# Three-layer relational graph convolution: two of three layers with more dense node ranges, gather ring of eight groups

## The chip, the cores and the metric

The kernel runs on one core of a Trainium2 chip. A core has TensorE (PE, matrix products; PEld is its weight load), VectorE (DVE), ScalarE (ACT), GpSimd (POOL) and SyncE (SP), which work in parallel and wait for each other through semaphores, and 16 DMA engines. The metric is the device time of one execution in microseconds (us); lower is better.

## The reference

There are 6250 nodes with 128 features, 100000 edges of four types, sorted by destination (the destinations are denser at low node numbers), and three layers:

```python
def _rgcn_conv(x, edge_index, edge_type, W, root, bias):
    src, dst = (edge_index[0], edge_index[1])
    x_src = x[src]
    out = x @ root + bias
    for r in range(N_REL):
        mask = (edge_type == r).astype(x.dtype)
        s = jax.ops.segment_sum(x_src * mask[:, None], dst, num_segments=N_NODES)
        c = jax.ops.segment_sum(mask, dst, num_segments=N_NODES)
        mean = s / jnp.maximum(c, 1.0)[:, None]
        out = out + mean @ W[r]
    return out
...
for l in range(N_LAYERS - 1):
    x = _rgcn_conv(x, edge_index, edge_type, weights[l], roots[l], biases[l])
    x = jax.nn.relu(x)
x = _rgcn_conv(x, edge_index, edge_type, weights[-1], roots[-1], biases[-1])
return x
...
x = _layernorm(x + _L0_gnn_ref(edge_index, edge_type_4, x, L0_gnn_weights, L0_gnn_roots, L0_gnn_biases), axis=-1)
```

## The kernel before

The edges lie in tiles of 128 and groups of four tiles, 196 groups in all, the nodes in 49 blocks of 128. A group's edges reach few nodes, since the destinations are sorted. There are two ways to sum a group.

**Sparse.** GpSimd fetches the rows of x times W for the edges of a tile by an indirect DMA (L724) from the table `ytab` in DRAM into `ring`, which holds `R` = 9 groups. Gather group n waits until TensorE has used group n - R (L720). VectorE builds the weighted one-hot matrices `S` (L1347), and TensorE multiplies (L888, items "S", eight matmul records to a group) into `psGR` or `psRB`. VectorE adds the sums to `node` (L1369, items "A").

**Dense.** The first groups, whose edges fall on few nodes, are put together to windows of at most 116 destination nodes. `WINDOWS` says how many windows each layer sums densely: 5, 9 and 9, that is groups 0 to 57 in the first layer and 0 to 76 in the others. A window's matrix A counts the edges between every source node and its destination nodes, per type. TensorE multiplies the split features `xs` by A (L970, 98 products of 512 columns to a window, items "C" in 25 pieces of two blocks), and then by the weights (L913, item "G"). Marker items in between are "M" (the counts broadcast by L905 and copied by ScalarE at L1081), and "F" (the product of both at L1500). A window is **built** in the first layer that uses it: bins from its edges (items "P": L1378 to L1382 on VectorE, L939 and L941 on TensorE), then per block one-hots (L1397, L1398 on VectorE), their product (L986) and a copy (L1070), and every two blocks a conversion to 16 bits (L1074) and a store to `a_dram`. In later layers the window is **loaded**: 13 chunks of up to 512 KB go through the two slots of `aring` (issue L630 on SyncE, after the slot's last chunk has been converted), and ScalarE converts each in two pieces (L1046) into `afull`. The first layer builds windows 0 to 4, the second loads these and builds 5 to 8, the third loads all nine. Loaded windows alternate between the banks `psD` and `psB` (the table `second`); built windows all use `psD`, since `psB` then holds the bins of the next one.

**Preparation.** Before the layers, VectorE ranks the edges of the windows in phases of about 100 tiles (`rank_counts`, `rank_scan`, `rank_places`, L1160 to L1215): windows 0, then 1 to 3, then 4 to 8. Behind the last phase it sets a flag (L1330), for which all engines wait in `branch`. Before the flag GpSimd gathers only the first R groups.

**What sets the order.** `schedule` writes one list of items per layer from planned costs, and all engines follow it in order. It takes `R`, the number of windows and their groups. A loaded piece of two blocks costs 0.88 us of TensorE in its table, which has no term for the loads. `pace` spreads the dense items so that they end some 100 us ahead of the gathers, and it is at least 1. Items "E" (the next layer's table, `relu` and `root` products) and "L" (the layer norm and output) go in between as soon as their nodes are complete. A layer's first gather waits until the table is stored (`y_stored`).

Of the kernel before, what the change touches and what calls it, by code (L numbers as in the profile page):

```python
# [17 lines left out]
P = 128  # L18
D = 128
NR = 4  # L20
# [1 line left out]
RW = 1024  # L22
FAR = 1000000
EPS = 1e-5
WINDOWS = (5, 9, 9)
SPAN = 116
START_PE, START_POOL = 205.0, 95.0
BANK = 4
# [5 lines left out]
class Plan:  # L34
# [3 lines left out]
    def __init__(self, N, E):  # L38
# [9 lines left out]
        g = 0  # L48
        while len(self.win) < max(WINDOWS):
            h = g  # L50
# [14 lines left out]

        self.W = [min(w, len(self.win)) for w in WINDOWS]
        self.G1 = [self.win[w - 1][1] for w in self.W]
# [40 lines left out]

def schedule(pl, R):

# [24 lines left out]
    for li in range(NL):  # L135
# [58 lines left out]
        def step_pool():  # L194
            nonlocal pool
            n = len(arrive)
            if n >= NS or (n >= R and n - R >= len(eaten)):
                return False
            pool = max(pool, eaten[n - R] if n >= R else 0.0) + ntile[n] * gather
            arrive.append(pool + land)  # L200
# [72 lines left out]
def rgcn_kernel(nc, x, src, dst, typ, weights, roots, biases, c_ident, c_iota, c_tri, c_col, c_need,  # L273
# [3 lines left out]
    NP, NG, NT, NB, NSL, TH = pl.NP, pl.NG, pl.NT, pl.NB, pl.NSL, pl.TH  # L277
    NT4 = NP * 8
    NW = NB * P + P
    NK = NR * N  # L280
    R = 9
    NS = 6
    SHEAD = 3
    YS = 4
# [6 lines left out]
    NPB = 2  # L291
# [13 lines left out]
    width = [c * NB for _, _, c in pl.win]  # L305
    layers = schedule(pl, R)

# [74 lines left out]
    with ctx:  # L382
        sb = lambda name, shape, dt=F32: ctx.enter_context(nc.sbuf_tensor(name, shape, dt))
# [36 lines left out]
        bt = sb("bt", [P, NL])  # L420
        ring = sb("ring", [P, R * 512])
        S = sb("S", [P, NS, 4, P])
# [11 lines left out]
        WB = W * NB  # L434
        OH = NO * (1 + NR) * P // 2
        PBW = P + max(width)
        V = sb("V", [P, max(NR * P + OH + NPB * 4 * PBW, 4 * WB + 5 * TH + 4 * (NP + 2))])
        cap, tot, offs, adj = (V[:, i * WB:(i + 1) * WB] for i in range(4))
        blk, tmpi, tmp2 = (V[:, 4 * WB + i * TH:4 * WB + (i + 1) * TH].bitcast(I32) for i in range(3))
        relw = V[:, 4 * WB + 3 * TH:4 * WB + 4 * TH]  # L440
        ident16 = V[:, 4 * WB + 4 * TH:4 * WB + 4 * TH + P // 2].bitcast(F16)
        rowt = V[0:2, 4 * WB + 5 * TH:4 * WB + 5 * TH + 4 * (NP + 2)].rearrange("r (a b c) -> r a b c", a=2, b=2)
        ms = V[:, 0:NR * P]
        oh = V[:, NR * P:NR * P + OH].bitcast(F16).rearrange("p (v c) -> p v c", v=NO)
        ohs, ohk = oh[:, :, 0:P], oh[:, :, P:(1 + NR) * P]
# [54 lines left out]
        q = {n: sem(n) for n in names}  # L500
        s_ring = [sem(f"s_ring{i}") for i in range(R)]
        s_yd = [sem(f"s_yd{i}") for i in range(YS)]
# [1195 lines left out]
```

## Time and profile before

| what | us |
|---|---|
| median of 3 runs | 2216.3 |
| their range | 2212.05 to 2216.36 |
| the profiled execution | 2218.82 |
| its span, first to last instruction | 2217.0 |
| GpSimd busy | 1556.1 (70%) |
| TensorE busy | 1591.0 (72%) |
| VectorE busy | 1239.0 (56%) |
| ScalarE busy | 1002.8 (45%) |

The span is that of one profiled execution; the profile's page gives busy times, the chain of work that ended last, and groups of instructions by source line. In a row, "<-" behind a bracketed number names what ended the idle time before the instruction; "issue" means that nothing in the profile held it. Busy time of TensorE counts pipelined products by modelled ends.

### The profile page before, as it was taken

The page shows a single profiled execution, that of the slowest core. Times are in us where ns is not written, and L with a number is a line of the kernel's source. Part 1 is how long each engine was busy: PE and PEld are TensorE (multiplying, and loading weights), DVE is VectorE, ACT ScalarE, POOL GpSimd, SP SyncE. Part 2 cuts the span into 40 slices and gives each one's busy share as a digit, 9 for nine tenths or more (in the row PEclk, how much of TensorE's full clock was granted, in tenths as well). Part 3 has the DMA queues.
Part 4 walks back from the last instruction along what each step waited for, and adds up shares of the span by engine and source line. Part 5 has one row for each costly group of instructions (what it writes and reads, how often), then busy time and mean ns, then how long its engine had stood idle before and what let it go on. Part 6 is the DMA issues. An engine that isn't in the chain of part 4 may idle for free.

```text
span 2217.0 us, 27610 instructions
## 1 busy us (share of the span) xinstructions
PE 1591.0 (72%) x7831; PEld 1130.9 (51%) x7831; DVE 1239.0 (56%) x4096; ACT 1002.8 (45%) x1499; POOL 1556.1 (70%) x1506
## 2 busy tenths in 40 slices
PE   6612768888898886558899887787476777777743
PEld 3301434555565554337677555554255566656532
DVE  4887988989876753223248766563133233433343
ACT  4400002446676771146667675683244454544200
POOL 0182887777777777747777777777477777777774
PEclk9855667989998996679999899998679988999855
DMA  6300122323444453257774444454465555656331
GB/s 206 136 29 18 59 67 73 115 97 133 134 160 136 162 172 112 86 189 231 218 222 149 142 156 133 151 173 146 126 216 169 168 181 178 198 186 188 119 87 49
DMA packets 164847, 314.28 MB, mean 142 GB/s; under 512 B 34816, under 2 KB 85120, under 8 KB 164692
## 3 DMA queue, kind: packets, MB, share of 16 engines
q1 hardware_dynamic: 113096, 210.74, 27.8%
q0 software_dynamic: 47936, 98.12, 15.9%
q10 hardware_dynamic: 3660, 3.60, 0.6%
q8 instruction: 67, 1.10, 0.2%
q14 instruction: 88, 0.72, 0.1%
HBM read 206.52 MB, written 105.80 MB: 141 GB/s over the span
## 4 chain that ended last, share of the span: by engine, by line
POOL 49%; issue 18%; DVE 15%; PE 9%; DMA 5%; ACT 1%; DVEq 1%; ACTq 1%; SPq 0%; POOLq 0%
POOL ring L724 49%; DMA aring<-a_dram 2%; PE psY L764 2%; DVE V L1398 2%; DVE S L1347 2%; DMA ring<-ytab,idxc 2%; DVE V L1397 2%; DVE V L1382 1%; PE psD L970 1%; DVE rows L1197 1%; PE psT L764 1%; PE psRB L888 1%; DVEq L1355 1%; ACT afull L1046 1%; DVE node L1369 1%
## 5 line engine op out<-in xcount | busy, mean ns | idle before, releaser
L724 POOL DMA_INDIRECT ring<-ytab,idxc x1498 | 1553.1, 1037 | 639.5 <-issue 449.0
L970 PE MATMUL psD<-afull,xs 128*128 128x512 f32 (+1 forms) x1666 | 572.8, 472 | 59.6 <-ACT afull L1046 33.1
L1347 DVE TENSOR_SCALAR S<-iota,relc,wc 128x128 f32<-128x128 f32 x1498 | 418.4, 365 | 114.5 <-PE psGR L888 74.3
L1046 ACT ACTIVATE afull<-aring 128x1024 fp32r<-128x1024 f16 (+1 forms) x350 | 346.0, 1032 | 213.7 <-DMA aring<-a_dram 139.1
L970 PEld LDWEIGHTS psD<-afull,xs 128*128 128x128 f32 (+1 forms) x1666 | 330.8, 205 | 130.0 <-issue 32.6
L888 PE MATMUL psRB<-S,ring 128*128 128x128 f32 x1516 | 246.3, 313 | 178.6 <-DMA ring<-ytab,idxc 171.4
L888 PE MATMUL psGR<-S,ring 128*128 128x128 f32 x1480 | 241.6, 316 | 175.5 <-DMA ring<-ytab,idxc 158.1
L888 PEld LDWEIGHTS psRB<-S,ring 128*128 128x128 f32 x1516 | 220.7, 220 | 219.2 <-issue 178.0
L888 PEld LDWEIGHTS psGR<-S,ring 128*128 128x128 f32 x1480 | 218.6, 223 | 213.7 <-issue 167.8
L1074 ACT ACTIVATE aring<-afull 128x1024 f16<-128x1024 f32 (+1 forms) x225 | 234.0, 1040 | 21.0 <-ACT afull L1070 0.7
L1070 ACT ACTIVATE afull<-psT 128x512 fp32r<-128x512 f32 x295 | 171.5, 593 | 115.7 <-PE psT L986 113.5
L1397 DVE TENSOR_SCALAR V<-iota,recs 128x128 f16<-128x128 f16 x588 | 157.4, 268 | 101.3 <-PE psT L986 58.2
L1398 DVE TENSOR_SCALAR V<-iota,recs 128x512 f16<-128x512 f16 x588 | 209.8, 357 | 0.0
L970 PE MATMUL psB<-afull,xs 128*128 128x512 f32 (+1 forms) x588 | 159.2, 416 | 6.0 <-ACT afull L1046 6.0
L986 PE MATMUL psT<-V 128*128 128x512 f16 x389 | 142.4, 405 | 6.5 <-DVE V L1398 6.3
L1369 DVE TENSOR_TENSOR node<-node,psRB 128x128 f32 x199 | 57.2, 287 | 154.6 <-issue 72.6
L1053 ACT ACTIVATE xs<-xst 128x512 fp32r<-128x512 f32 (+1 forms) x39 | 23.2, 595 | 266.2 <-DMA xst<-in_x 243.9
L1369 DVE TENSOR_TENSOR node<-node,psGR 128x128 f32 x200 | 57.4, 287 | 126.7 <-DVE node L1369 63.1
L970 PEld LDWEIGHTS psB<-afull,xs 128*128 128x128 f32 (+1 forms) x588 | 110.6, 198 | 31.1 <-ACT afull L1046 7.8
L999 ACT ACTIVATE yst<-psT 128x512 f32<-128x512 f32 x66 | 39.2, 595 | 185.0 <-PE psT L764 184.9
L1070 ACT ACTIVATE afull<-psY 128x512 fp32r<-128x512 f32 x146 | 86.4, 592 | 61.6 <-PE psY L986 60.8
L764 PE MATMUL psY<-wt,node 128*128 128x512 f32 (+1 forms) x162 | 94.9, 671 | 22.4 <-DVE node L1487 14.1
(197 smaller groups left out, 1470.4 us busy)
## 6 DMA issues: line engine op xcount, KB each, us to landing
aring<-a_dram SPq DMA_DIRECT2D x168, 512.0 KB
a_dram<-aring SPq DMA_DIRECT2D x108, 512.0 KB
ytab<-yst SPq DMA_DIRECT2D x144, 256.0 KB
ring<-ytab,idxc POOLq DMA_INDIRECT x1498
hrows<-yst SPq DMA_DIRECT2D x96, 64.0 KB
xst<-hrows SPq DMA_DIRECT2D x24, 256.0 KB
xst<-in_x SPq DMA_DIRECT2D x12, 256.0 KB
yst<-in_x SPq DMA_DIRECT2D x11, 256.0 KB, 4.2
```

The costliest lines, as they stand in the source:

```text
L724: e.indirect_dma_start(ring[0:m, at:at + P], None, Y[li % 2], bass.IndirectOffsetOnAxis(ap=idxc[0:m, t:t + 1], axis=0)).then_inc(s_ring[n ...
L764: e.matmul(y_bank(li, k)[0:bw[k], :], h, wt[:, li].rearrange("i r o -> i (r o)"), start=True, stop=True).then_inc(q["s_ym"], 1)
L888: last = e.matmul(o, ring[0:m, at:at + P], S[0:m, n % NS, i, :], start=(i == 0), stop=(i == len(tiles[g]) - 1))
L970: last = e.matmul(bank[:], xs[0:m, s, i, :], a, start=(i == 0 and s == 0), stop=(i == NB - 1 and s == 1))
L986: e.matmul(tbank(u)[:], ohs[:, v % NO, :], ohk[:, v % NO, :], start=(j == 0), stop=(j == c - 1)).then_inc(q["s_bd"], 1)
L1046: e.activation(afull[:, n % AF, 0:m, :], aring[:, cc % AS, o:o + m, :], ACT.Copy).then_inc(q["s_cv"], 1)
L1070: e.activation(afull[:, n % AF, j, :], tbank(u)[:], ACT.Copy).then_inc(q["s_tA"], 1)
L1074: e.activation(aring[:, cc % AS, half:half + m, :], afull[:, n % AF, 0:m, :], ACT.Copy).then_inc(q["s_cv"], 1)
L1347: last = e.tensor_scalar(S[:, n % NS, i, :], iota[:], relc[:, t:t + 1], wc[:, t:t + 1], ALU.is_equal, ALU.mult)
L1369: e.tensor_tensor(w, w, part[bank][:, j * P:(j + 1) * P], ALU.add).then_inc(q["s_acc"], 1)
L1397: e.tensor_scalar(ohs[:, v % NO, :], iota16[:, 0:P], recs[:, 0, at:at + 1], None, ALU.is_equal)
L1398: e.tensor_scalar(ohk[:, v % NO, :], iota16[:], recs[:, 1, at:at + 1], None, ALU.is_equal).then_inc(q["s_oh"], 1)
```

## The change

The dense windows become 5, 10 and 13, and the ring 8 groups. With `SPAN` unchanged the new windows are windows 9 to 12, which hold groups 77 to 80, 81 to 84, 85 to 88 and 89 to 91. The first layer still uses windows 0 to 4. The second loads 0 to 4 and builds 5 to 9; the third loads 0 to 9 and builds 10 to 12. Sparse groups are 138, 115 and 104 instead of 138, 119 and 119; tiles 550, 458 and 414 instead of 550, 474 and 474. The edges of windows to be ranked grow from 308 to 368 tiles, and the preparation has a fourth phase with windows 9 to 12. The rest of the diff packs `ident16` and `rowt` closer in the buffer `V`.

```diff
-WINDOWS = (5, 9, 9)
+WINDOWS = (5, 10, 13)
...
-    R = 9
+    R = 8
...
-        V = sb("V", [P, max(NR * P + OH + NPB * 4 * PBW, 4 * WB + 5 * TH + 4 * (NP + 2))])
+        V = sb("V", [P, max(NR * P + OH + NPB * 4 * PBW, 4 * WB + 4 * TH + P // 2 + 4 * (NP + 2))])
...
-        rowt = V[0:2, 4 * WB + 5 * TH:4 * WB + 5 * TH + 4 * (NP + 2)].rearrange("r (a b c) -> r a b c", a=2, b=2)
+        rowt = V[0:2, 4 * WB + 4 * TH + P // 2:4 * WB + 4 * TH + P // 2 + 4 * (NP + 2)].rearrange("r (a b c) -> r a b c", a=2, b=2)
```

On VectorE, in the preparation behind the third ranking phase (L1213 is its last step, L1312 the first step towards the flag), the difference of the two orders begins so:

```order
 L1213 SCALAR_TENSOR_TENSOR colc<-V 128x16
+L1165 MEMSET rows 128x1470
+L1166 TENSOR_TENSOR rows<-V,iota 128x2940
+L1171 TENSOR_REDUCE V<-rows 128x49 x4
+L1185 COPY V<-psGR 128x196
+L1186 TENSOR_TENSOR V<-V 128x196
+L1188 TENSOR_TENSOR V<-psGR,V 128x196
+L1192 TENSOR_TENSOR V<-V 128x195
+L1194 CAST rows<-V 128x49 x4
+L1197 SCALAR_TENSOR_TENSOR rows<-rows 128x2940
+L1198 TENSOR_TENSOR rows<-rows 128x2940
```

A whole phase is added, over 60 tiles (2940 = 49 x 60), between the third and the flag.

On TensorE, in the third layer, from the product by the weights for one loaded window (L913) towards the next window's counts (L905), before:

```order
L913 MATMUL psGR<-V,wt 128x128 x4
L888 MATMUL psRB<-S,ring 128x128 x4
L970 MATMUL psD<-afull,xs 128x512 x8
L888 MATMUL psRB<-S,ring 128x128 x4
L970 MATMUL psD<-afull,xs 128x512 x12
L888 MATMUL psRB<-S,ring 128x128 x4
L970 MATMUL psD<-afull,xs 128x512 x12
L888 MATMUL psRB<-S,ring 128x128 x4
L970 MATMUL psD<-afull,xs 128x512 x8
```

And after, at the same place of the layer:

```order
L913 MATMUL psRB<-V,wt 128x128 x4
L888 MATMUL psRB<-S,ring 128x128 x4
L970 MATMUL psD<-afull,xs 128x512 x20
L888 MATMUL psRB<-S,ring 128x128 x4
L970 MATMUL psD<-afull,xs 128x512 x16
L888 MATMUL psRB<-S,ring 128x128 x4
L970 MATMUL psD<-afull,xs 128x512 x20
```

Between two gather groups (L888) there stand 16 to 20 dense products (L970) where 8 to 12 stood. From one window's counts to the next there are six groups instead of eleven: M0 to M9 stand at groups 4, 10, 16, 22, 28, 33, 39, 45, 51 and 57, where M0 to M8 stood at 11, 22, 33 and so on to 96. In the second layer M4 moves from group 34 to group 30.

## Rows read from the trace of the kernel before

**Rows 1.** Page, the chain that ended last, share of the span by engine.
```profile
POOL 49%; issue 18%; DVE 15%; PE 9%; DMA 5%; ACT 1%; DVEq 1%; ACTq 1%; SPq 0%; POOLq 0%
```

**Rows 2.** Waits of GpSimd: us in total, times, longest us.
```profile
POOL ring L724 <- issue: 449.0, 1473, 0.3
...
POOL ring L724 <- PE psGR L888: 42.5, 8, 40.3
```

**Rows 3.** Gathers alone, first layer: length, POOL busy (instructions), clock, DMA share, GB/s.
```profile
220.00:941.00 721.00, 564.18 (x514) 0.84 0.36 115
```

**Rows 4.** Timeline, GpSimd, at the layers' ends: start, us, instruction, [idle <-releaser].
```profile
220.45 1.50 POOL L724 DMA_INDIRECT ring<-ytab,idxc  x1 [40.33 <-PE psGR L888]
...
964.35 0.95 POOL L724 DMA_INDIRECT ring<-ytab,idxc  x1 [23.37 <-DMA hrows<-yst]
...
1575.70 0.87 POOL L724 DMA_INDIRECT ring<-ytab,idxc  x1 [0.30 <-issue]
1601.65 0.95 POOL L724 DMA_INDIRECT ring<-ytab,idxc  x1 [25.09 <-DMA hrows<-yst]
...
2195.36 0.87 POOL L724 DMA_INDIRECT ring<-ytab,idxc  x1 [0.30 <-issue]
```

**Rows 5.** Timeline, third ranking phase in the preparation, VectorE and TensorE.
```profile
169.60 2.10 DVE L1165 MEMSET rows<- 128x2450 uint32 x1 [0.58 <-DVE colc L1213]
171.62 5.20 DVE L1166 TENSOR_TENSOR rows<-V,iota 128x4900 uint8<-128x4900 int32 x1
176.86 5.50 DVE L1171 TENSOR_REDUCE V<-rows 128x49 f32<-128x1176 uint8 x5
...
187.10 10.37 DVE L1197 TENSOR_TENSOR_SCAN rows<-rows 128x4900 f16<-128x4900 f16 x1
197.50 5.26 DVE L1198 TENSOR_TENSOR rows<-rows 128x4900 f16<-128x4900 f16 x1
202.88 4.27 PE L808 MATMUL psGR<-rows,V 128*128 128x100 f16 x49 [18.42 <-DVEq L1199]
...
208.21 0.54 DVE L1213 SCALAR_TENSOR_TENSOR colc<-V 128x24 f32<-128x24 int32 x5
```

**Rows 6.** Timeline, ScalarE, second layer: the marks of windows 0, 1, 2, 4.
```profile
1013.40 0.60 ACT L1081 ACTIVATE V<-psT 128x512 f32<-128x512 f32 x1 [2.92 <-PE psT L905]
...
1049.02 0.58 ACT L1081 ACTIVATE V<-psT 128x512 f32<-128x512 f32 x1
...
1087.65 0.58 ACT L1081 ACTIVATE V<-psY 128x512 f32<-128x512 f32 x1
...
1170.65 0.60 ACT L1081 ACTIVATE V<-psY 128x512 f32<-128x512 f32 x1 [0.62 <-PE psY L905]
```

**Rows 7.** Chain within 1010 to 1070: shares; then start us, us, what.
```profile
by line: DMA aring<-a_dram 54.0%; ACT afull L1046 20.5%; issue 15.7%; PE psD L970 5.9%; PE psT L905 1.8%; ACT xs L1053 1.1%; PE psRB L888 0.7%; ACTq L1045 0.2%; ACT V L1081 0.0%; ACTq L1097 0.0%; ACTq L1080 0.0%
...
1036.63 3.55 DMA aring<-a_dram
...
1041.17 1.05 ACT afull L1046
1042.24 4.33 DMA aring<-a_dram
```

**Rows 8.** Windows: length, busy PE, PEld, DVE, ACT, POOL, clock, DMA share, GB/s.
```profile
1049.00:1088.00 39.00, 33.06 (x162) 25.97 (x161) 9.22 (x33) 25.38 (x28) 29.55 (x32) 0.96 0.70 217
...
1602.00:2196.00 594.00, 410.66 (x2006) 334.17 (x2007) 204.36 (x753) 236.33 (x259) 449.84 (x474) 0.84 0.53 163
```

**Rows 9.** Timeline, TensorE: two blocks of a built window; a group and loaded products.
```profile
1384.85 0.40 PE L986 MATMUL psY<-V 128*128 128x512 f16 x1
...
1385.55 0.39 PE L986 MATMUL psT<-V 128*128 128x512 f16 x1
...
1699.72 1.13 PE L888 MATMUL psGR<-S,ring 128*128 128x128 f32 x8 [1.90 <-DMA ring<-ytab,idxc]
1700.61 3.02 PE L970 MATMUL psB<-afull,xs 128*128 128x512 f32 x12
```

## The prediction

> **What bounds the kernel now.** I read the page's chain first. GpSimd's gathers (L724) hold 49% of it, and most of the 18% called "issue" is the pause between two gathers [rows 1]. The waits of GpSimd come next: 449.0 us in 1473 pauses of at most 0.3 us are its own stepping. Waits on TensorE are 8 with 42.5 us, of which 40.3 us is the single one before the restart at 220.45 [rows 2]. So after the restart the gathers never waited for a free ring group.
>
> That makes the span a sum over GpSimd [rows 3, 4]: the preparation to 220.45, the first layer's 514 remaining tiles in 721 us (1.40 us a tile), a gap of 23.4 us, the second layer's 474 tiles from 964.35 to 1576.57 (612.2 us, 1.29 a tile), a gap of 25.1 us, the third layer's 474 tiles from 1601.65 to 2196.23 (594.6 us, 1.25 a tile), and 20.8 us of tail. A group of four tiles costs the gather queue 5.0 us in the third layer.
>
> The question is whether the dense work of a layer can keep that pace, so I then read the one stretch in which loaded windows follow each other as fast as they can: the start of the second layer. Its five loaded windows are marked by the copies of the broadcast counts (L1081): 1013.40, 1049.02, 1087.65 and, two windows on, 1170.65 [rows 6]. The first mark comes 49 us after the layer's first gather, the next gaps are 35.6 and 38.6 us, the last two average 41.5 us and hold other work. The chain there is not the gathers but load, conversion, load: 54% of it is aring<-a_dram, with loads of 3.55 and 4.33 us [rows 7]. Two ring slots of 512 KB and two conversions of about 1.0 us for each chunk give about (3.8 + 2.0) / 2 = 2.9 us for a chunk, and 13 chunks make a window of 37.7 us, which the two clean gaps (mean 37.1) bear out. TensorE is close behind: 33.06 us busy in 39 [rows 8].
>
> **The change, part by part.**
>
> Gathers removed. The second layer drops groups 77 to 80, 16 tiles: 16 x 1.25 = 20 us off GpSimd. The third drops groups 77 to 91, 60 tiles: 60 x 1.25 = 75 us. If GpSimd stayed the bound everywhere, this would be the gain.
>
> Preparation. Four more windows form a fourth ranking phase, 60 tiles long, on VectorE, and it stands before the flag for which all engines wait [rows 5]. The third phase (100 tiles, five windows) took from 169.60 to 208.78, 39.2 us. Clear, compare, reduce, scan and multiply (2.10 + 5.20 + 5.50 + 10.37 + 5.26 = 28.4 us) go with tiles times blocks, so x0.6: 17.1. The 49 products (4.27) have a floor; I take 3.7. The other 6.5 us goes with the four windows and fixed steps: 5.9. Sum 26.7 us, plus 1 us for longer record operations (308 to 368 columns). Nothing covers it: GpSimd had filled its ring and stood idle for 40.33 us before the restart [rows 4]. Bounds: 22 (all of it x0.6) and 39 (as long as the third phase).
>
> Ring of eight. GpSimd has 32 instead of 36 tiles gathered before the restart, so four more follow the restart, where one took 1.50 us and its pause of 0.3 [rows 4] and later ones 1.25 in all: 6 us. Elsewhere the ninth group is only lead. In the gather order of the first layer nothing else changes.
>
> Second layer. One more window is built. The one-hots of built windows slow the gathers: the second layer took 17.6 us longer than the third with as many tiles and four built windows [rows 4], so 4.4 us each. The five loaded windows are now laid against 31 groups up to F4 instead of 35, while they load no faster. TensorE starts group 30 after M4, at about 203 us (206.3 before, less the products of four groups, partly hidden). With eight ring groups GpSimd may then be in its 38th or 39th group; at 5.15 us a group it would have been near its 40th. I take a stall of 7 us (0 to 15). Net: -20 + 4.4 + 7 = -9 us. Later TensorE has 14 or 15 groups to a built window where it had 17; a block takes 0.70 us [rows 9], 34 us a window, and it has room.
>
> Third layer. Here the order runs ten loaded windows in 58 groups: M0 stands at group 4, M9 at group 57, 5.9 groups or 29.5 us a window. The second excerpt of the order shows six gather groups in a window where there were eleven. No stretch of the trace has a loaded window below 35.6 us [rows 6]. TensorE executes in order, so groups wait behind dense products, and GpSimd, eight groups ahead at most, waits for it. M9 comes at 49 + 9 x 37.1 = 383 us into the layer, group 57 at 386. GpSimd can have issued 65 groups by then (alone it would have done so at 326): a stall of 60 us. From there 39 groups with 154 tiles remain, 154 x 1.247 = 192 us, plus 3 x 4.4 = 13 us for three built windows. Last gather at 386 + 205 = 591 us, against 594.6: the layer gains 4 us, not 75. During those 205 us TensorE has three built windows (3 x 34 us of blocks, 3 x 8 us of counting and turning) and 46 groups x 1.13 us [rows 9], 178 us in all: it catches up, with little to spare. I leave gaps and tail as they are.
>
> Sum: 26.7 + 1 + 6 - 9 - 4 = +21 us. Span 2217.0 to about 2238. The profiled execution took 2218.82, 2.5 over the median of the runs, 2216.3; I add 20 us to the median: 2236.
>
> How fast a load can be is the widest term, and a page speaks to it. The rows show 3.55 to 4.33 us for 512 KB [rows 7]. The Trainium skill, "DMA: Bandwidth & Descriptors", section "Anatomy of one DMA", gives 2.0 us fixed plus bytes at 436 GB/s; as an estimate this is 3.2 us a load, (3.2 + 2.0) / 2 x 13 = 34 us a window, and the sum would be -7 instead of +21. The rows were taken beside the gathers and decide for now.
>
> **Rivals.**
>
> *Thinner gathers let the loads run faster.* While GpSimd stalls, its group comes every 6.2 us (six in a window) instead of 5, and the loads share the DMA engines, busy 0.70 there [rows 8], with less. TensorE's own floor is 98 products x 0.252 = 24.7 us (twelve take 3.02) and six groups x 1.13 = 6.8 us [rows 9], with turns about 33 us. At 33 to 34 us M9 comes at 346 to 355, the last gather at 554 to 563, and the sum is -16 to -7: 2200 to 2209, faster. It decides from a window of 34.7 us downwards, where the sum is zero. For it: the page above. Against: 35.6 us is the best of any window, while gathers took their 5 us.
>
> *The gathers stay the bound.* Then the stall is none, the third layer gains 75 - 13 = 62 us and the second 16: 28 + 6 - 16 - 62 = -44, 2172. It needs windows of 29.5 us, under TensorE's floor of 31.5. Against it stands arithmetic; for it only that TensorE had idle time all through the third layer (410.66 us busy in 594) before [rows 8].
>
> *TensorE falls behind as well.* Loaded windows of 39 to 41 us (the second layer's average with everything in it is 39.3), built windows that need 66 instead of 59 us because three follow each other on one bank, and a lag carried over the end of the second layer, which lengthens the gap: +17 to +35 in loading, +10 to +20 in the rest. Sum about +50 to +70: 2265 to 2286.
>
> *The change doesn't do what it says.* The counts of gathers and windows are fixed by the code; I see no way.
>
> **How the numbers follow.** Forecast (windows of 35 to 39 us, sum +2 to +38) 0.63; faster loads 0.16; gathers the bound 0.05; TensorE behind 0.16. The range leaves out the last two's ends and the bottom of faster loads: 2202 to 2266. A measurement of this kernel can tell about 0.2% (4.4 us) from no change. Faster than 2212 takes a window under 34.3 us or a cheaper preparation: 0.18. Within 4.4 us: windows near 35: 0.09. Slower: 0.73.
>
> **What would show it.** In the new profile GpSimd's restart lies at 247 to 250. GpSimd waits for TensorE (L888) some 60 us in the third layer, most of it in its first 390 us, and 0 to 15 us in the second. The third layer's marks of L1081 lie 36 to 39 us apart for loaded windows, with ScalarE waiting on aring<-a_dram at nearly each chunk, and the last gather comes 575 to 605 us after the layer's first. The forecast is wrong if GpSimd waits for nothing there, if the marks are under 34 us apart, or if the preparation grows by much under 22 us.

## The result and the profile after

The changed kernel takes 2248.8 us (median of 4 runs, 2244.99 to 2255.12) against 2216.3 us before. The ratio is 1.0154, with a 95% interval of 1.0127 to 1.0181: slower, as forecast, and a little slower than the 2236 us of the forecast. The profiled execution took 2244.99 us, the lowest of the four, with a span of 2243.1 us, so all that follows explains 26.1 us between the two spans. The profile before lay 2.5 us above its median and this one lies 3.8 us below its own: 6.4 of the 32.5 us between the medians stay without a row.

GpSimd's timeline gives the sum again, as [rows 4] did. Columns are start, duration, instruction, and idle time before it with what ended it:

```profile
248.92 1.50 POOL L724 DMA_INDIRECT ring<-ytab,idxc  x1 [80.02 <-PE psGR L888]
...
964.69 0.87 POOL L724 DMA_INDIRECT ring<-ytab,idxc  x1 [0.30 <-issue]
...
987.62 0.95 POOL L724 DMA_INDIRECT ring<-ytab,idxc  x1 [22.07 <-DMA hrows<-yst]
...
1591.43 0.87 POOL L724 DMA_INDIRECT ring<-ytab,idxc  x1 [0.30 <-issue]
...
1616.72 0.95 POOL L724 DMA_INDIRECT ring<-ytab,idxc  x1 [24.43 <-DMA hrows<-yst]
...
2211.78 0.87 POOL L724 DMA_INDIRECT ring<-ytab,idxc  x1 [0.30 <-issue]
```

| stretch | before | after | difference | forecast |
|---|---|---|---|---|
| preparation, to the restart | 220.5 | 248.9 | +28.5 | +27.7 |
| first layer, restart to last gather | 720.5 | 716.6 | -3.9 | +6 |
| gap | 23.4 | 22.1 | -1.3 | 0 |
| second layer | 612.2 | 604.7 | -7.5 | -9 |
| gap | 25.1 | 24.4 | -0.7 | 0 |
| third layer | 594.6 | 595.9 | +1.3 | -4 |
| tail | 20.8 | 30.4 | +9.6 | 0 |

The differences add up to 26.0 us, the forecasts to 20.7.

The third layer has 60 gathers fewer and is no shorter. What GpSimd waited for there (us in total, times), from the source view of L724 from 1616 to 2213:

```profile
  issue: 112.8, 370
  PE psGR L888: 45.7, 21
  PE psRB L888: 30.9, 22
```

Those 43 waits on TensorE are new. Before, a wait on TensorE in the layers was the ordinary pause of 0.3 us; less 0.3 us each, the new ones sum to 63.6 us. Of the marks of the third layer's windows (ScalarE's timeline; answers to [rows 6]) these are M0, M1, M2, M8 and M9, and then the three built windows:

```profile
1666.34 0.60 ACT L1081 ACTIVATE V<-psT 128x512 f32<-128x512 f32 x1 [3.97 <-PE psT L905]
...
1703.06 0.57 ACT L1081 ACTIVATE V<-psY 128x512 f32<-128x512 f32 x1
...
1740.29 0.57 ACT L1081 ACTIVATE V<-psT 128x512 f32<-128x512 f32 x1
...
1970.91 0.60 ACT L1081 ACTIVATE V<-psY 128x512 f32<-128x512 f32 x1 [0.16 <-PE psY L905]
...
2010.60 0.58 ACT L1081 ACTIVATE V<-psT 128x512 f32<-128x512 f32 x1
...
2069.02 0.58 ACT L1081 ACTIVATE V<-psY 128x512 f32<-128x512 f32 x1
...
2132.34 0.58 ACT L1081 ACTIVATE V<-psY 128x512 f32<-128x512 f32 x1
...
2190.21 0.58 ACT L1081 ACTIVATE V<-psY 128x512 f32<-128x512 f32 x1
```

M0 comes 49.6 us into the layer; nine windows take 344.3 us, 38.3 each, where the order had 29.5. The built ones come 58 to 63 us apart. The chain from 1670 to 2000 is the load chain of [rows 7], now for 330 us on end:

```profile
by line: DMA aring<-a_dram 58.7%; ACT afull L1046 19.0%; issue 14.8%; PE psD L970 5.1%; PE psGR L888 0.8%; PE psRB L888 0.5%; PE psB L941 0.4%; PE psB L939 0.3%; ACTq L1045 0.3%; PE psRB L913 0.3%; ACT sd L1085 0.1%; ACTq L1080 0.0%
```

The second layer shows the same in small: 14 waits on TensorE, 8.9 us beyond the ordinary pause, most of them between groups 24 and 36.

### The profile page after: what moved, and what is told of

Its sections match the earlier page's. It is cut to its first block, busy times and chain, and to the rows that moved or that the text cites. A ratio compares the mean times of both kernels' runs of the same rounds, so it can differ in the third digit from the quotient of the medians.

```text
span 2243.1 us, 30353 instructions
## 1 busy us (share of the span) xinstructions
PE 1716.7 (77%) x8626; PEld 1194.3 (53%) x8626; DVE 1369.2 (61%) x4544; ACT 1229.8 (55%) x1825; POOL 1484.0 (66%) x1430
## 4 chain that ended last, share of the span: by engine, by line
POOL 25%; DVE 21%; PE 17%; DMA 14%; issue 14%; ACT 7%; DVEq 1%; ACTq 1%; SPq 0%
POOL ring L724 25%; DMA aring<-a_dram 13%; PE psD L970 5%; ACT afull L1046 4%; DVE S L1347 3%; DVE V L1398 3%; DVE V L1397 2%; DVE rows L1197 2%; PE psGR L888 2%; PE psY L764 1%; ACT afull L1070 1%; DVE V L1382 1%; PE psT L986 1%; DVE node L1369 1%; PE psRB L888 1%
## 5 line engine op out<-in xcount | busy, mean ns | idle before, releaser
L724 POOL DMA_INDIRECT ring<-ytab,idxc x1422 | 1481.0, 1041 | 728.0 <-issue 412.4
L970 PE MATMUL psD<-afull,xs 128*128 128x512 f32 x2058 | 699.2, 463 | 80.0 <-ACT afull L1046 42.5
L970 PEld LDWEIGHTS psD<-afull,xs 128*128 128x128 f32 x2058 | 390.3, 197 | 174.1 <-ACT afull L1070 43.9
L1074 ACT ACTIVATE aring<-afull 128x1024 f16<-128x1024 f32 (+1 forms) x325 | 338.1, 1040 | 30.4 <-ACT afull L1070 1.1
L1070 ACT ACTIVATE afull<-psT 128x512 fp32r<-128x512 f32 x430 | 247.5, 591 | 121.4 <-PE psT L986 119.2
L1398 DVE TENSOR_SCALAR V<-iota,recs 128x512 f16<-128x512 f16 x784 | 282.7, 361 | 0.0
L888 PE MATMUL psGR<-S,ring 128*128 128x128 f32 x1448 | 218.5, 301 | 75.9 <-DMA ring<-ytab,idxc 59.1
L888 PE MATMUL psRB<-S,ring 128*128 128x128 f32 x1396 | 213.2, 301 | 73.2 <-DMA ring<-ytab,idxc 71.2
L1397 DVE TENSOR_SCALAR V<-iota,recs 128x128 f16<-128x128 f16 x784 | 214.2, 273 | 84.3 <-PE psT L986 57.9
L888 PEld LDWEIGHTS psGR<-S,ring 128*128 128x128 f32 x1448 | 204.5, 212 | 94.9 <-issue 78.0
L888 PEld LDWEIGHTS psRB<-S,ring 128*128 128x128 f32 x1396 | 197.5, 211 | 96.7 <-issue 73.5
L970 PE MATMUL psB<-afull,xs 128*128 128x512 f32 x686 | 186.7, 416 | 52.8 <-ACT afull L1046 39.8
L970 PEld LDWEIGHTS psB<-afull,xs 128*128 128x128 f32 x686 | 124.2, 194 | 97.3 <-ACT afull L1046 33.0
L1369 DVE TENSOR_TENSOR node<-node,psRB 128x128 f32 x189 | 54.4, 288 | 122.1 <-DVE node L1369 59.7
L1369 DVE TENSOR_TENSOR node<-node,psGR 128x128 f32 x196 | 56.4, 288 | 115.1 <-DVE node L1369 59.8
L1382 DVE SCALAR_TENSOR_TENSOR V<-iota,colc,vals 128x98 f16<-128x98 f16 (+2 forms) x368 | 118.4, 384 | 0.0
```

Source lines behind the costliest of these rows:

```text
L724: e.indirect_dma_start(ring[0:m, at:at + P], None, Y[li % 2], bass.IndirectOffsetOnAxis(ap=idxc[0:m, t:t + 1], axis=0)).then_inc(s_ring[n ...
L888: last = e.matmul(o, ring[0:m, at:at + P], S[0:m, n % NS, i, :], start=(i == 0), stop=(i == len(tiles[g]) - 1))
L970: last = e.matmul(bank[:], xs[0:m, s, i, :], a, start=(i == 0 and s == 0), stop=(i == NB - 1 and s == 1))
L1070: e.activation(afull[:, n % AF, j, :], tbank(u)[:], ACT.Copy).then_inc(q["s_tA"], 1)
L1074: e.activation(aring[:, cc % AS, half:half + m, :], afull[:, n % AF, 0:m, :], ACT.Copy).then_inc(q["s_cv"], 1)
L1369: e.tensor_tensor(w, w, part[bank][:, j * P:(j + 1) * P], ALU.add).then_inc(q["s_acc"], 1)
```

## The experiments

Nine kernels, three of which ran twice. The first four shared a chip on which the kernel before took 2215.9 us.

**The ring alone.** The kernel before with

```diff
-    R = 9
+    R = 8
```

> The kernel before with the ring of eight groups alone (windows 5, 9, 9). My theory (the ring is only lead; four gathers more stand behind the flag): +6 us, 2222 us, GpSimd waits for TensorE nowhere in the layers, not even at the second layer's loaded windows where the lead fell to 10 us with nine groups. Rival (the ninth group covers the loaded windows): a stall of 10 to 20 us in the second layer, 2230 to 2240 us.

Measured: 2216.3 us, ratio 0.9998 (0.9984 to 1.0012). The restart is at 221.44, the first layer takes 718.7 us with its four more gathers (720.5 before), the second 612.5, the third 595.5. So the smaller ring costs nothing by itself, and next to nothing at the second layer's loaded windows (0.7 us of stall). My term of +6 was wrong. Four gathers at 1.25 us should still be 5 us; in all four kernels of this chip the first layer has 518 tiles behind the restart and takes 718.7 to 721.8 us, as long as 514 tiles took. That the stretching of gathers there comes from VectorE's work, which is the same amount in either case, would fit; no run shows it. Nor does one show why the kernel after needs 2 to 5 us less than these four (716.6).

**The preparation alone.** The kernel after, whose windows go back to 5, 9 and 9 while thirteen are ranked:

```diff
-WINDOWS = (5, 10, 13)
+WINDOWS = (5, 9, 9)
+RANKED = 13
...
-        while len(self.win) < max(WINDOWS):
+        while len(self.win) < RANKED:
```

> Windows 5, 9, 9 and a ring of eight, but all thirteen windows are ranked in the preparation, so the fourth ranking phase is there and nothing uses it. My theory: it costs its own 27 to 29 us in full, whatever follows: 28 us over the kernel with the ring of eight alone, about 2250 us. Rival (part of it is hidden by gathers or by waits behind the flag): 10 to 20 us over it. If this holds, the layers of the changed kernel together gave nothing back.

Measured: 2242.2 us, ratio 1.0115 (1.0090 to 1.0140), 25.9 us over the ring alone. GpSimd's restart with the ring of eight, and with the preparation added:

```profile
221.44 1.50 POOL L724 DMA_INDIRECT ring<-ytab,idxc  x1 [52.87 <-PE psGR L888]
```

```profile
247.98 1.50 POOL L725 DMA_INDIRECT ring<-ytab,idxc  x1 [79.44 <-PE psGR L889]
```

The restart moves by 26.5 us, GpSimd's idle time before it grows by as much, and all of it reaches the end: no cover. This one term is as large as the whole difference of the spans: in the changed kernel the layers and gaps gave back 12.1 us, of which the tail took 9.6.

**The second layer's window, without built ones in the third.**

```diff
-WINDOWS = (5, 10, 13)
+WINDOWS = (5, 10, 10)
```

> Windows 5, 10, 10, ring of eight: one window more is built in the second layer and loaded in the third, none is built in the third. My theory: ring +6, a short ranking phase of 16 tiles +12, second layer -8 (20 of gathers less the one-hots and a stall of 7), third layer -20 since its loaded windows are 9 groups apart (46 us, above the 38 us that a load needs), no stall, tail unchanged: -10, 2206 us. Rival (each dense window costs the layer what its gathers gave): second 0, third 0, +18, 2234 us.

Measured: 2199.7 us, ratio 0.9919 (0.9894 to 0.9945), faster than both kernels; the 6 us under the forecast are the ring's term, which is nothing here either. Restart at 232.89 (+12.4), second layer 606.4 us (-5.8, stall 11.4), third layer 574.7 us (-19.9), tail 19.6. In the third layer the source view of L724 from 1605 to 2180 has

```profile
  issue: 136.8, 449
  DMA hrows<-yst: 23.8, 1
  PE psGR L888: 1.2, 4
  PE psRB L888: 1.2, 4
```

Eight waits of the ordinary 0.3 us: no stall, though ten windows are loaded as in the kernel after. Their order has them 9 groups apart instead of 5.9, and their marks lie 42 to 48 us apart. So it is not the number of loaded windows, but how closely the order sets them, that makes GpSimd wait.

**The third layer's windows, without the second's.**

```diff
-WINDOWS = (5, 10, 13)
+WINDOWS = (5, 9, 13)
```

> Windows 5, 9, 13, ring of eight: the second layer as before, the third loads nine and builds four. My theory: ring +6, preparation +28, second layer 0, third layer: M8 at 49 + 8 x 38.25 = 355 us with group 51, 59 groups issued, then 178 tiles x 1.247 + 4 x 4.4 = 240 us, 595 to 600 us where 594.6 stood, tail +15 because the dense items end behind the last gather group: +50, 2266 us. Rival (no load bound, the gathers set the third layer): 594.6 - 75 + 18 = 537, tail +10, about 2202 us.

Measured: 2266.5 us, ratio 1.0224 (1.0199 to 1.0249), the forecast by the load bound. That it is so to the microsecond is luck: the profiled execution lay 4 us lower, the first two layers came out 9 us below their terms, and the preparation and the tail some 4 us above. The third layer takes 596.0 us (40 waits on TensorE, 57.8 us beyond the ordinary pause); M0 to M8 come 36.2 to 44.5 us apart, mean 38.6. The tail is 38.2 us: the last dense items of this order stand behind the last gather group.

**What makes a loaded window 38 us.** The other five fell, in two sittings, on two other chips: in the first sitting the kernel before takes 2524.5 us, in the second 2497.4. GpSimd, VectorE and ScalarE show pauses there which the profile puts down to "remote" (157.8 us on GpSimd in small4's second sitting), which the first chip's profiles don't have; their cause stays open. The kernel after did not run on these chips. So absolute times below are compared only within a sitting, and the marks, which are the point, with those of the kernel after.

Chunks of one piece, 256 KB, in four slots (the same buffer and the same bytes); the indices `it[2] // 2`, `kc // 2` and `p // 2` of a chunk become those of the piece:

```diff
-CH, PIECE, TAHEAD = 4, 2, 3
+CH, PIECE, TAHEAD = 2, 2, 3
...
-    AS = 2
+    AS = 4
```

> The changed kernel with chunks of one piece (256 KB) in four slots: the same bytes, the same buffer, twice the loads. My theory (a loaded window takes 38 us because only two loads are in turn with their conversions): the marks of loaded windows come 33 to 35 us apart, TensorE's own pace, the stall of 64 us in the third layer falls to 10 to 25, the layer takes 545 to 565 us instead of 596, the 9 us in the second go, the tail goes back to about 21: 2195 to 2210 us. Rival (the DMA engines' bandwidth beside the gathers sets it): marks stay 37 to 38 apart, 2245 to 2250 us.

> small4 again. Its first run fell on a chip where the kernel before took 2524 us, with pauses on all engines that the first chip did not show; there the marks of loaded windows lay 35 us apart. On a chip where the kernel before takes 2216: marks 33 to 35 apart, third layer's stall 10 to 25 us, the layer 555 to 570 us, the second layer's stall gone, tail 21 to 25: 2200 to 2215 us. Rival (the gain shows only where everything else is slow): 2245 to 2250 us.

Loads of half the partitions (the other 64 keep what an earlier window left there, so the sums are not the layer's):

```diff
-                e.dma_start(aring[:, cc % AS, 0:len(pl.chunks[k]), :], a_view(w, k)).then_inc(s_as[cc % AS], 16)
+                e.dma_start(aring[0:P // 2, cc % AS, 0:len(pl.chunks[k]), :], a_view(w, k)[0:P // 2]).then_inc(s_as[cc % AS], 16)
```

> The changed kernel, but each load brings only the upper 64 of 128 partitions, half of the bytes (the rest of the matrix is left as an earlier window left it). Both theories on loads: the marks come 33 to 35 us apart, 2195 to 2210 us; if small4 stays slow and this one is fast, bytes decide, and if both are fast, it is the turn of the slots. Rival (TensorE or ScalarE's conversions set the pace): no change, 2245 to 2250 us.

> halfload again (each load brings 64 of 128 partitions; the rest of the matrix is left as it was), on a chip of the first kind. Its first run had loads of 3.7 us in the chain, as long as whole ones, and marks 38 us apart, against both of my theories on loads. Revised theory: a load costs its start and completion, not its bytes, so two slots give the same 37 to 38 us a window and the same 2240 to 2250 us. Rival (bytes decide, and the slow chip covered it): 2195 to 2215 us.

One of two dense products left out:

```diff
-                for s in range(2):
-                    last = e.matmul(bank[:], xs[0:m, s, i, :], a, start=(i == 0 and s == 0), stop=(i == NB - 1 and s == 1))
+                for s in range(1):
+                    last = e.matmul(bank[:], xs[0:m, s, i, :], a, start=(i == 0 and s == 0), stop=(i == NB - 1))
```

> The changed kernel with one of the two dense products of a block left out (the low part of the split features), which halves TensorE's dense work, 24.7 to 12.4 us a window. My theory (loads set the pace): the marks of loaded windows stay 36 to 38 us apart, the third layer's stall stays 50 to 64 us; only the built windows and the tail gain, 2225 to 2240 us. Rival (TensorE sets the pace): marks 26 to 30 us apart, no stall, third layer 530 to 540 us, 2165 to 2180 us.

| kernel | us | ratio to before (95%) | M0 to M9, us a window | third layer, us | tail, us |
|---|---|---|---|---|---|
| after (first chip) | 2248.8 | 1.0154 (1.0127 to 1.0181) | 38.3 | 595.9 | 30.4 |
| small4 | 2517.8 | 0.9973 (0.9943 to 1.0003) | 35.8 | 630.0 | 48.4 |
| halfload | 2550.7 | 1.0105 (1.0036 to 1.0175) | 38.4 | 648.8 | 47.3 |
| onesplit | 2519.1 | 0.9978 (0.9950 to 1.0007) | 38.6 | 650.2 | 49.1 |
| small4, second sitting | 2496.8 | 0.9998 (0.9962 to 1.0035) | 35.2 | 628.5 | 48.8 |
| halfload, second sitting | 2536.4 | 1.0123 (1.0071 to 1.0175) | 38.2 | 660.7 | 45.7 |

Three readings. With half of the dense products the loaded windows keep 38.6 us and the third layer its length (650.2 us, halfload 648.8), while the first two layers of onesplit are 11 and 20 us shorter than those of halfload: TensorE doesn't set the pace of loaded windows. The experiment is weaker than its edit looks. In onesplit's loaded windows (1885 to 2232) the granted clock was 0.82, a mean over its two levels of 1.2 and 2.4 GHz, where the kernel after had 0.98 (1670 to 2000), and a product took 0.48 to 0.50 us in the median instead of 0.39; TensorE's busy share fell only from 87% to 73%. Its chain there speaks for the same reading: 44.4% loads, 16.5% conversions, 4.6% dense products.

With half of the bytes the loaded windows keep 38.4 and 38.2 us: the bytes don't either, and the expectation that both theories on loads shared was wrong.

With the same bytes in twice as many loads in flight they fall to 35.8 and 35.2 us, and the kernel takes 33 and 40 us less than halfload of the same sitting, which has to stand in for the kernel after. In the second layer small4's loaded windows are no shorter than those of the kernel after on its chip (M0 to M4: 39.2 us a window in both sittings, 38.4 there).

Chain by line in the loaded windows, halfload (second sitting, 1905 to 2240), then small4 (second sitting, 1880 to 2190):

```profile
by line: DMA aring<-a_dram 31.6%; issue 27.9%; ACT afull L1046 13.0%; PE psD L970 11.2%; PE psB L970 4.0%; SPq L630 2.3%; PE psRB L888 2.2%; PE psGR L888 1.1%; another core or an unknown queue 1.0%; PE psB L941 0.7%; PE psB L939 0.6%; DVE S
```

```profile
by line: PE psD L970 25.1%; PE psB L970 21.3%; issue 15.8%; ACT afull L1046 8.6%; PE psGR L888 5.2%; DMA aring<-a_dram 4.7%; PE psRB L888 4.7%; another core or an unknown queue 4.1%; PE psT L905 1.8%; DVE S L1347 1.7%; PE psRB L913 1.4%; DV
```

With four slots the loads nearly leave the chain (4.7% for 31.6%; in the first sitting 10.3% for 30.1%) and TensorE's dense products take it, at the 35 us that are close to its own work: it is busy 283.7 of those 310 us. The loads in the chain of halfload last 3.7 us in the median (second sitting 3.6), those of onesplit, whole ones in halfload's first sitting, 3.7, those of the kernel after 3.7. So in the kernel after two slots in turn with their conversions, each load at a length that didn't follow its bytes, fit a window's 38 us: loads and conversions are 77.7% of its chain. In halfload they are only 44.6% and "issue" is 27.9%, so what holds its windows at 38 us is less clear.

That a load of 64 partitions used fewer DMA engines, which would hide an effect of bytes, the packet records of the traces speak against: of the loads whose packets stand apart from other loads', those of 64 partitions have 16 to 20 packets under way at their fullest, those of 128 have 17 to 20. The packets of such a load take about 1.5 us from the first to the last in halfload and 2.2 us in onesplit and in the kernel after, so this part did follow the bytes; what fills the rest of a load's 3.6 to 3.7 us is not shown. And small4 changes two things at once: there are more loads in flight, and a slot comes free after one conversion instead of two. The runs don't separate these.

What small4 did not do is what I had expected of it beyond the marks: the third layer's stall was still 42.5 and 51.9 us (halfload 80.6 and 102.8, onesplit 83.1, where I had expected 50 to 64) and the tail 48 us. The built windows lie 71 to 82 us apart on these chips, where the first chip had 58 to 63; that this keeps the stall and the tail would fit and is not shown. The time on the first chip, where I put it at 2200 to 2215 us, was not measured.

**Windows 5, 10 and 10 with four slots.** The diffs of second and small4 together.

> Windows 5, 10, 10 with chunks of one piece in four slots. My theory: against windows 5, 10, 10 with two slots (2199.7 us) only the second layer's stall of 11 us goes, since the third layer had none: 2188 us. Rival (twice as many DMA issues on SyncE and smaller packets delay the table stores): 2200 us or more.

> Windows 5, 10, 10 with four slots of one piece, again. Only the second layer's stall of 11 us and nothing else goes against the same windows with two slots (2199.7 us): 2186 to 2192 us. Rival (smaller packets and twice the issues cost more than that): 2200 us or more.

Measured: 2517.8 and 2488.4 us, ratios 0.9974 (0.9945 to 1.0002) and 0.9966 (0.9940 to 0.9993). A gain of about a quarter and a third of a per cent over the kernel before there, the first not clear of the noise; tail 24.5 and 23.3 us. The same windows with two slots did not run on these chips. Whether four slots add to windows 5, 10, 10 on the first chip is not settled.

**Windows 5, 10 and 11 with four slots.** The same with `WINDOWS = (5, 10, 11)`.

> Windows 5, 10, 11 with four slots of one piece. The third layer loads ten windows 7 groups apart (35 us, just what four slots give) and builds one. Against 5, 10, 10: 16 gathers fewer in the third layer, -20 us, one-hots +4.4, ranking of 32 instead of 16 tiles +5: -11, 2178 us. Rival (35 us is too tight, groups wait behind dense products again): stall of 10 to 20 in the third layer, 2190 to 2200 us.

Measured: 2478.6 us, ratio 0.9913 (0.9884 to 0.9943), 9.8 us under windows 5, 10, 10 of the same sitting, near the 11 us expected. The loaded windows of the third layer come 37 to 47 us apart, there is a stall of 26.3 us, above the 10 to 20 of its rival, and the layer takes 644.8 us against 661.5.

## Why the prediction was right, and where it was not

The direction and the two large terms, the preparation and the third layer's bound, were right in mechanism. That the sum of the spans, +21 for +26.1, is so close is luck in part: the first layer came out 9.9 us below its term and the tail 9.6 us above, and the two cancel. What is left, 5 us, is nearly all the third layer.

**The preparation: right.** +27.7 forecast, +28.5 in the profile, 25.9 when alone. The argument by the third phase's rows [rows 5] and GpSimd's idle 40.33 us [rows 4] held: idle time in front of the restart covers nothing that moves the restart.

**The ring: wrong, and small.** The four gathers that stand behind the flag cost 0 and not 6 us (ring8). What I got right is that no stall comes of the lost ninth group by itself.

**The second layer: right.** -7.5 for -9, stall 8.9 us for 7. The run with windows 5, 10, 10 has it again: -5.8 and 11.4.

**The third layer: right in mechanism, a few us off in two terms.** Windows of 38.3 us for 37.1; two clean gaps had given the 37.1, the nine now range from 36.7 to 41.4. M9 came at 393.9 us for 383, the stall was 63.6 us for 60. From M9 to the last gather it took 202 us for 208. That loads and not TensorE set the pace was an argument then; onesplit and small4 bear it out, on other chips.

**The Trainium skill's price of a load ("DMA: Bandwidth & Descriptors", section "Anatomy of one DMA"): the measurement decides against it.** The 34 us a window that the prediction estimated from it would have given -7 us in sum. The trace has 3.72 us in the median (49 loads of the chain from 1670 to 2000, 3.32 to 5.85) instead of 3.2, and the sum went by the rows. The section gives this price for DMAs that GpSimd issues, and these loads are SyncE's, which the prediction passed over. Half of the bytes should have made a load 0.6 us shorter by it, as an estimate; in the medians of the chains halfload's loads (3.73 and 3.61 us) show no such difference.

**The tail: wrong.** "I leave gaps and tail as they are" failed by 9.6 us in the tail; the gaps held within 1.3. Of the rival in which TensorE falls behind as well, this is akin to its lag, but at the third layer's end; its slower windows did not come (loaded 38.3 us, built 57.9 to 63.3). After the last window's sum (L913) stand the layer norms of the nodes that wait for it. In the changed kernel this is the timeline of 2196 to 2236, of which these are the last window's product and the first steps of the norms (L1419):

```profile
2197.09 1.16 PE L913 MATMUL psRB<-V,wt 128*128 128x128 f32 x8 [0.78 <-DVE V L1500]
...
2213.12 0.69 DVE L1419 TENSOR_TENSOR yst<-psT,yst 128x512 f32<-128x512 f32 x1 [1.63 <-PE psT L920]
...
2216.74 0.68 DVE L1419 TENSOR_TENSOR yst<-psT,yst 128x512 f32<-128x512 f32 x1
...
2220.35 0.69 DVE L1419 TENSOR_TENSOR yst<-psY,yst 128x512 f32<-128x512 f32 x1
...
2228.66 0.69 DVE L1419 TENSOR_TENSOR yst<-psT,yst 128x512 f32<-128x512 f32 x1 [1.21 <-PE psT L920]
...
2232.28 0.68 DVE L1419 TENSOR_TENSOR yst<-psT,yst 128x512 f32<-128x512 f32 x1
...
2235.90 0.28 DVE L1419 TENSOR_TENSOR yst<-psY,yst 106x128 f32<-106x128 f32 x1
```

and in the kernel before, from its last gather (2196) on:

```profile
2203.14 0.69 DVE L1419 TENSOR_TENSOR yst<-psT,yst 128x512 f32<-128x512 f32 x1 [1.21 <-PE psT L920]
...
2206.76 0.75 DVE L1419 TENSOR_TENSOR yst<-psY,yst 128x384 f32<-128x384 f32 x2
```

A norm of four blocks takes 3.6 us. Before, the last window's mark was at 2087.84, 108 us ahead of the last gather, and two norms were left after it. Now it is 22 us ahead, five such norms and one of a single block come behind the last gather, and the final sums queue between them on VectorE. Before, the final sums (L1369) started at 2199.39, 3.2 us behind the last gather. Now TensorE has made the last group's products by 2215.5, but VectorE has three norms first and starts these sums at 2223.96, 11.3 us behind the last gather: 8.1 of the 9.6 us. That the tail goes with how late the last window ends is what the runs of the first chip agree on: 20.8 and 20.6 us with its mark 108 us ahead (before, prep; ring8 likewise), 19.6 at 108 us (second), 30.4 at 22, 38.2 with the mark 1 us behind the last gather (third).

**Rivals.** That the gathers stay the bound fell with the 63.6 us of waits on TensorE. That thinner gathers speed the loads fell with the marks: 38.3 us a window although a group came only every 6.2 us. "It does what it says" was never in doubt.

## What to carry to other kernels

Before work is moved from one engine to a path that is idle on average, find the tightest stretch in which that path already runs, and take its pace from there: an order written from planned costs keeps a promise only for what its costs contain, and here they had no term for the loads. Work in front of a flag on which every engine waits is paid in full, however idle the engines are, and it can eat the gain of a change that is sound behind it. When windows of work are packed to the end of a stage, look at what waits for the last one.

## What was not expected

A load of 512 KB and one of 256 KB in 64 partitions took about as long from issue to landing (3.72 us, and 3.67 on the chip of halfload's first sitting; 3.73 and 3.61 us, all medians of the chains). Two such loads in flight gave a window of 13 chunks in 38.3 us, four of half the size in 35.2 to 35.8 us with the same bytes, on other chips. Halving the dense products took only 14 points off TensorE's busy share, as the granted clock went from 0.98 to 0.82. And one fewer group in the gather ring changed nothing, in a kernel whose lead over TensorE had at its narrowest been 10 us.
